# Last stage: the layer norm ahead of the feed-forward part with tokens on partitions, and call lists in another order

## The reference

```python
for i in range(DEPTH):
    x = attn_layer(shift_tokens(x), Wqkv[i], q_scale[i], k_scale[i], Wo[i]) + x
    x = ffn_layer(shift_tokens(x), ln_g[i], ln_b[i], W1[i], b1[i], W2[i], b2[i]) + x

def attn_layer(x, Wqkv, qs, ksc, Wo):      # 16 heads of 64
    q, k, v = split_heads(x @ Wqkv)
    q, k = l2norm(q) * qs, l2norm(k) * ksc
    q, k = rotary(q), rotary(k)            # with position scales
    out = local_attention(q, k, v)         # windows of 32, each sees itself and the one before
    return out @ Wo

def ffn_layer(x, g, bln, W1, b1, W2, b2):
    mu = x.mean(-1, keepdims=True)
    var = ((x - mu) ** 2).mean(-1, keepdims=True)
    xn = (x - mu) / jnp.sqrt(var + 1e-05) * g + bln
    a, gate = jnp.split(xn @ W1 + b1, 2, -1)
    return a * jax.nn.gelu(gate, approximate=False) @ W2 + b2
```

## Time and profile before

| | us |
|---|---|
| median of 3 runs | 4661.67 |
| lowest and highest | 4660.33 and 4680.19 |
| span of the profiled execution, first to last instruction | 4655.4 |

### The profile page before, as it was taken

The page is one execution under the profiler, slowest core; times in us unless marked ns, Lnnn a source line. Parts: engine busy times, 40 slices in busy tenths (PEclk is TensorE's granted clock), DMA queues, the critical chain, the costliest instruction groups (busy, mean ns, idle before and its releaser), DMA issues.

```text
span 4655.4 us, 137933 instructions
## 1 busy us (share of the span) xinstructions
PE 4360.4 (94%) x56640; PEld 2936.9 (63%) x56640; DVE 3703.2 (80%) x5128; ACT 3238.4 (70%) x6002; POOL 3648.6 (78%) x1951
## 2 busy tenths in 40 slices
PE   7889899978887999999999999999999999999998
PEld 4556688854443666666666666666666666666665
DVE  6874476759997888888888788888888788878885
ACT  4666655657774777777777777777777777777775
POOL 2223344469997999988999899989999898989993
PEclk9999999989998999999999999999999999999999
DMA  2000000023331222322233322323223222322222
GB/s 81 2 2 2 2 1 1 1 110 146 146 146 57 67 63 61 80 65 66 58 70 74 71 63 61 79 66 69 58 67 76 69 64 60 78 68 66 59 68 53
DMA packets 164376, 290.47 MB, mean 62 GB/s; under 512 B 44063, under 2 KB 61350, under 8 KB 159654
## 3 DMA queue, kind: packets, MB, share of 16 engines
q1 hardware_dynamic: 162310, 281.40, 23.2%
q10 hardware_dynamic: 1440, 0.24, 0.0%
HBM read 90.16 MB, written 2.62 MB: 20 GB/s over the span
## 4 chain that ended last, share of the span: by engine, by line
PE 57%; issue 4%; DVE 4%; DMA 2%; ACT 1%; SPq 1%; POOL 0%; DVEq 0%; ACTq 0%
PE ps L2626 19%; PE ps L2682 7%; PE ps L2639 7%; PE ps L2694 7%; PE ps L2655 5%; PE ps L2668 3%; PE ps L2720 3%; PE ps L2736 3%; PE ps L2727 3%; DMA L3f_vw<-L3f_v 2%; DVE L3f_ss L3019 1%; PE ps L2701 1%; PE ps L2707 1%; DVE L3f_raw L3036 1%; SPq L2472 1%
## 5 line engine op out<-in xcount | busy, mean ns | idle before, releaser
L3219 POOL TENSOR_TENSOR L3f_t<-L3f_raw,L3f_rot 128x1024 f32<-128x1024 f32 x384 | 1085.3, 2826 | 246.4 <-DVE L3f_raw L3036 242.8
L2626 PE MATMUL ps<-L3f_wqkv,all_z 128*128 128x512 f32 x2304 | 1154.1, 607 | 11.2 <-DVE L3f_raw L3036 8.8
L3236 POOL TENSOR_TENSOR L3f_raw<-L3f_raw,L3f_t 128x1024 f32<-128x1024 f32 x384 | 911.9, 2375 | 7.5
L3228 POOL TENSOR_TENSOR L3f_raw<-L3f_raw,L3f_rot 128x1024 f32<-128x1024 f32 x384 | 909.0, 2367 | 7.5
L2835 ACT ACTIVATE L3f_sqr<-ps 128x512 f32<-128x512 f32 x768 | 453.1, 595 | 295.8 <-PE ps L2626 292.4
L3036 DVE TENSOR_TENSOR L3f_raw<-ps,L3f_ri 128x512 f32<-128x512 f32 x768 | 498.7, 686 | 163.5 <-ACT L3f_ri L2845 154.4
L3019 DVE TENSOR_REDUCE L3f_ss<-L3f_sqr 128x8 f32<-128x512 f32 x768 | 515.6, 679 | 115.6 <-ACT L3f_sqr L2835 112.3
L2639 PEld LDWEIGHTS ps<-all_ident,L3f_raw 128*128 128x128 f32 x3072 | 363.3, 141 | 307.8 <-issue 270.3
L2626 PEld LDWEIGHTS ps<-L3f_wqkv,all_z 128*128 128x128 f32 x2304 | 395.8, 192 | 234.8 <-issue 180.2
L2639 PE MATMUL ps<-all_ident,L3f_raw 128*128 128x128 f32 x3072 | 474.5, 277 | 9.4 <-POOL L3f_raw L3236 3.7
L2682 PEld LDWEIGHTS ps<-L3f_pT,L3f_vw 128*64 128x64 f32 x12288 | 375.3, 138 | 97.0 <-issue 78.6
(11 more groups left out here) (332 smaller groups left out, 8632.4 us busy)
## 6 DMA issues: line engine op xcount, KB each, us to landing
L3f_vw<-L3f_v SPq DMA_DIRECT2D x1344, 128.0 KB, 2.4
L3a_Bs<-L3a_rows SPq DMA_DIRECT2D x16, 2048.0 KB, 7.1
L3a_Cs<-L3a_rows SPq DMA_DIRECT2D x16, 2048.0 KB, 11.7
L3f_vw<-L3f_v SPq DMA_DIRECT2D x192, 64.0 KB
L3f_wqkv<-in_L_ffn_Wqkv SPq DMA_DIRECT2D x24, 256.0 KB, 4.3
L3f_wqkv<-in_L_ffn_Wqkv SPq DMA_DIRECT2D x6, 512.0 KB, 4.2
L3f_wo<-in_L_ffn_Wo SPq DMA_DIRECT2D x48, 64.0 KB, 2.4
out<-all_x SPq DMA_DIRECT2D x8, 256.0 KB, 3.2
```

The source lines that it names most:

```text
L2626: p.matmul(PS[:, j % 3, :], Z[:, u % NSEQ, t * P:t * P + P], w, start=True, stop=True).then_inc(proj.sem)
L3219: g.tensor_tensor(t.rearrange("p h (b e) -> p h b e", b=2), r.rearrange("p h (b e) -> p h b e", b=2)[:, :, ::-1, :], w[:, 1, :].rearrange( ...
L3228: g.tensor_tensor(r, r, w[:, 0, :].unsqueeze(1).broadcast_to((P, H, HD)), ALU.mult).then_inc(cosined.sem)
L3236: g.tensor_tensor(r, r, t, ALU.add).then_inc(rotated.sem)
```

## The change

The norm ahead of the feed-forward part is computed with tokens on partitions. `turn_z` transposes the unit's two tiles of Z into the second half of bank 4; VectorE takes statistics (`stats`, `bn_stats` on each tile) and aggregates them into mean and variance per token (`moments`, `bn_aggr`); ScalarE takes logarithm and exponential of two values per partition (`root`); VectorE subtracts the mean and scales, both as values per partition (`normal`, two instructions, from PSUM into `zn`); `turn_n` transposes back into the same half bank; `affine` reads it from there. The constants `cmat` and `mean`, the products `centre` and `variance` and the square `centred` go. `turn_p` of the next unit now waits for `affine`. All call lists are in another order; the pairs of `pe` and `dve` are cut at another place of the period (`pe` now starts at `project_out(2i)`, `dve` at `residual(2i)`), and `pool` is written one pair ahead, with `add` of the odd unit's "q1" behind `sine` of its "k1". The diff, cut to its core:

```diff
-            def centre(u):
-                p.wait_ge(*z_attn.at(u))
-                p.matmul(PS[:, 4, SEQ:2 * SEQ], cmat[:, :], Z[:, u % NSEQ, 0:SEQ], start=True, stop=True).then_inc(c_mm.sem)
-            def variance(u):
-                p.wait_ge(*c_sq.at(u))
-                p.matmul(PS[:, 5, 0:SEQ], mean[:, :], xq[:, :], start=True, stop=True).then_inc(v_mm.sem)
+            def turn_z(u):
+                p.wait_ge(*z_attn.at(u))
+                for t in range(TILES):
+                    mm = p.transpose(PS[:, 4, SEQ + t * P:SEQ + (t + 1) * P], Z[:, u % NSEQ, t * P:(t + 1) * P], ident[:, :])
+                mm.then_inc(y_turned.sem)
+            def turn_n(u):
+                p.wait_ge(*y_n.all(u))
+                for t in range(TILES):
+                    mm = p.transpose(PS[:, 4, SEQ + t * P:SEQ + (t + 1) * P], zn[:, t, :], ident[:, :])
+                mm.then_inc(n_turned.sem)
...
-                    p.wait_ge(*fn_n.at(u - 1))
+                    p.wait_ge(*fn_in.at(u - 1))
...
             def root(u):
+                a.wait_ge(*y_mv.all(u))
+                a.activation(zls[:, :], zmv[:, :, 1], ACT.Ln, bias=self.eps[:, :]).then_inc(y_ln.sem)
+                a.wait_ge(*y_ln.at(u))
+                a.activation(zrs[:, :], zls[:, :], ACT.Exp, scale=-0.5).then_inc(y_rs.sem)
             def affine(u):
-                a.wait_ge(*fn_n.at(u))
+                a.wait_ge(*n_turned.at(u))
-                a.activation(fn[:, (u % 2) * SEQ:(u % 2 + 1) * SEQ], rs[:, :], ACT.Identity, bias=gb[:, y, 1:2], scale=gb[:, y, 0:1]).then_inc(fn_in.sem)
+                a.activation(fn[:, (u % 2) * SEQ:(u % 2 + 1) * SEQ], PS[:, 4, SEQ:2 * SEQ], ACT.Identity, bias=gb[:, y, 1:2], scale=gb[:, y, 0:1]).then_inc(fn_in.sem)
...
+            def stats(u):
+                    v.bn_stats(zst[:, t, :], PS[:, 4, SEQ + t * P:SEQ + (t + 1) * P]).then_inc(y_st.sem)
+            def moments(u):
+                    v.bn_aggr(zmv[:, t, :], zst[:, t, :]).then_inc(y_mv.sem)
             def normal(u):
-                v.tensor_tensor(rs[:, :], PS[:, 4, SEQ:2 * SEQ], rs[:, :], ALU.mult).then_inc(fn_n.sem)
+                    v.tensor_scalar(zn[:, t, :], PS[:, 4, SEQ + t * P:SEQ + (t + 1) * P], zmv[:, t, 0:1], zrs[:, t:t + 1], ALU.subtract, ALU.mult).then_inc(y_n.sem)
```

More of the change, by code:

```diff
@@ L2753, in turn_back @@
                     mm.then_inc(z_turned.sem)
+            project_out(2 * i)
+            ffn_gate(2 * i - 1, 1)
+            ffn_up(2 * i - 1, 0)
+            ffn_gate(2 * i - 1, 2)
+            project(2 * i + 2, "v1b")
+            turn_z(2 * i)
+            project(2 * i + 3, "q0a")
+            ffn_up(2 * i - 1, 1)
+            ffn_up(2 * i - 1, 2)
+            project(2 * i + 3, "q0b")
+            project(2 * i + 3, "k0a")
+            turn_qk(2 * i + 2, 0, 0)
+            turn_back(2 * i - 1, range(FINAL - 1))
+            ffn_out(2 * i - 1)
+            turn_back(2 * i - 1, range(FINAL - 1, FINAL))
+            turn_qk(2 * i + 2, 0, 1)
+            project(2 * i + 3, "k0b")
+            turn_n(2 * i)
+            turn_qk(2 * i + 2, 0, 2)
+            project(2 * i + 3, "v0a")
+            turn_qk(2 * i + 2, 0, 3)
+            turn_p(2 * i + 1, 0)
             turn_qk(2 * i + 2, 1, 0)
-            scores(2 * i + 2, 0)
             project(2 * i + 3, "v0b")
@@ L2778, in pe @@
             project(2 * i + 4, "k0a")
-            centre(2 * i + 1)
+            turn_z(2 * i + 1)
+            project(2 * i + 4, "k0b")
+            project(2 * i + 4, "v0a")
             turn_qk(2 * i + 3, 1, 0)
-            project(2 * i + 4, "k0b")
-            variance(2 * i + 1)
-            project(2 * i + 4, "v0a")
+            turn_n(2 * i + 1)
             scores(2 * i + 3, 0)
@@ L3160, in dve @@
             scale(2 * i + 1, 0)
-            total(2 * i + 1, 1)
-            residual(2 * i)
+            share(2 * i + 1, 1)
+            stats(2 * i)
             gated(2 * i - 1, 0)
+            moments(2 * i)
             gated(2 * i - 1, 1)
```

281 lines of the change are left out of this document (133 added, 148 removed).

## The result

The changed kernel takes 4687.75 us (median of 7 runs, 4677.23 to 4696.77), the kernel before beside it 4661.67 (7 runs, 4647.66 to 4680.19): ratio 1.0061, 95% interval 1.0041 to 1.0080. It is 0.6% slower. The prediction was 4634.5, 0.6% faster; the range, up to 4688.0, just holds the median, and that is luck: its upper end was set for short stalls of TensorE, which hardly came. The profiled execution has a span of 4691.6 us against 4655.4, 36.2 us apart where the medians are 26.1 apart.

What follows compares the result with a forecast made beforehand. TensorE's instruction stream was taken as the bound (63.79 us busy of a 63.98 us pair). Terms: -41.7 saving, +12 stalls, +10.5 layer boundaries, -8 rotation tables, sum -27: 4661.7 to 4634.5 us, range 4604 to 4688.

Steps and rivals of the forecast that it cites:

- The bound and the saving: TensorE's instruction stream bounds the last stage; products removed less transposes added save 0.87 us per pair, 41.7 us in all.
- New stalls: Short new TensorE waits in the new order, taken as 0.25 us per pair, 12 us in all; bounds -14 to +67.
- (a): VectorE's work after project_out(2i), up to the norm freeing the PSUM bank for "v0a": some 0.4 us in hand.
- (b): Between turn_z(2i+1) and turn_n(2i+1): statistics, root and scalings must fit into 2.15 us; stall 0 to 0.4 us.
- (c): turn_p(2i+1, 0) now waits for affine instead of normal, whose bank it overwrites; stall 0 to 0.3 us.
- second rival: TensorE's gain is given back in short waits at (a), (b) and (c): 43 us of stalls, 4665 us; chance 0.29.
- Rotation tables: Table preparation on VectorE, five times, now right before residual(2i): costs 1.5 instead of 3.1 us each, -8 us in all.
- Layer boundaries: At 5 boundaries project_out waits for output weights, 2.1 us longer each: +10.5 us; bounds 0 and +20.
- The failed step: Each of four softmax scalings per pair waits on VectorE for the rest of one GpSimd instruction, 0 to 2.2 us.
- third rival: Softmax scalings' waits for GpSimd decide: two of 2.2 us per pair, mean scaling up 0.3 us, 4733 us; chance 0.12.
- None of this has a price by itself: Changed loads of VectorE, ScalarE and GpSimd cost nothing, as none passes 63.1 us per pair; only order can cost.
- fourth rival: Longer transpose runs bring one slow clock stretch per pair on TensorE, 1.9 us each, 91 us: 4725 us; chance 0.03.

Runs made afterwards that it cites:

- new_norm_old_order: Kernel before with only the new norm (transposes, VectorE statistics); old call lists, only the new steps have new places: 4867.34 us, ratio 1.0438.
- a_pool_behind: Changed kernel with one more GpSimd wait: ahead of sine(2i+3, "k1") it waits until scale(2i+2, 0) is done: 4652.75 us, ratio 0.9982.
- the pads: Tiny transposes ahead of the stage: 32 or 64 on the changed kernel with scale(2i+1, 1) later, 4739.57 and 4727.70 us; 64 on the kernel before, 4658.84.
- a_behind_apart: a_pool_behind with scores(2i+2, 0) put back ahead of the products v0b, q1a, q1b on TensorE: 4798.37 us, ratio 1.0289.
- b_close: Kernel before with scores(2i+2, 0) moved behind the products v0b, q1a, q1b on TensorE: 4736.62 us, ratio 1.0165.
- n_tuned: new_norm_old_order with scale(2i, 0) three places ahead of residual(2i-1), root and normal earlier, turn_p(2i+3, 0) one turn later: 4704.45 us, ratio 1.0089.
- n_tuned_behind: n_tuned with GpSimd waiting for scale(2i, 0) ahead of sine(2i+2, "q0"): 4699.40 us, ratio 1.0085.

## Why the prediction was wrong, step by step

- **The bound and the saving** were right. An undisturbed pair took 63.8 us and takes 62.4 to 62.9 now. The steps cost what their rows said. Statistics took 0.284 us and aggregates 0.171; the two new scalings took 0.404 each where I had 0.281, and that did no harm. Most undisturbed pairs lie under 62.7, which by my own sign makes the prediction wrong: I had not seen that the wait of `turn_p` for `normal`, 10.6 us in all, would go.
- **New stalls at (a), (b), (c), +12 us**: over-sized. Between 1500 and 4550 us `turn_n` waits 0.8 us in all, `turn_z` about 2, and the projections 3.7 us in 4 places for a norm. So the second rival did not come, in these lists; new_norm_old_order shows how real it is where the list gives a chain no room.
- **Rotation tables, -8**: from W to W the five such pairs took 66.72 to 71.34 us before. They take 62.95, 67.29, 63.52, 65.57 and 63.75 now, the second and fourth with 2.6 and 2.4 us of fetch waits in them. Each had a wait at the residual, 0.9 to 2.5 us; one of 0.4 us is left. An estimate from these rows, fetch waits and the shorter ordinary pair taken off, is -10: right.
- **Layer boundaries, +10.5**: +7.0 in waiting. W behind the wait takes 5.2 to 6.4 us in four boundaries and 3.7 in one, where before it took 5.2 to 5.4 in each.
- **The failed step** is the sentence that each scaling waits "for the rest of a GpSimd instruction, 0 to 2.2 us". The earlier trace rows show one such case, and I made it the upper end. In the changed lists GpSimd often runs eight and more instructions without a break (each starts before the one ahead of it has ended) when `scale(2i+2, 0)` asks. Of some 42 scalings that met such a run, 8 lost the path to two to four further instructions; of some 230 in the two kernels that met a run of up to six, none did. This one mis-sized term cost 35 us (a_pool_behind), and it is the third rival's mechanism: the two engines' lock decides; but not by its price, two scalings of 2.2 us in every pair, and not by its sign that the mean would rise by 0.3 us (it rose by 0.17). With 0.12 its chance was too low, because I judged it by means and not by what a rare long one does. "None of this has a price by itself", said of GpSimd's unchanged work too, is where I stopped asking.
- **The missing term** is fetch. The waits view of before shows 32.8 us of TensorE waiting for issue at `scores` alone, nearly twice the 17.6 us at the layer boundaries, which I priced. I took the 80 us of idle in the stage for 0.19 us per pair, from one undisturbed window. Fetch grew by 20 us, and with the lower clock behind each wait it ate most of what was left of the gain: without the scalings the kernels are equal.
- **The clock**: "fourth rival, 0.03" was right for undisturbed pairs, at 1.00 with 24 groups of transposes and four more pairs of them. The price came another way: each wait is followed by products at a lower granted clock (0.95 over the pair of 69.90 us), and 41 us of removed work became 16.7 of busy time. I had counted waits at their own length only. The Trainium skill, "TensorE: Matmul & The Clock Gate", section "Part 4: PE-mode transpose", has transposes not count as busy for the clock; no undisturbed pair of this kernel shows that (clock 1.00 over 62.60 us), with more of them than before.

The Trainium skill, "SBUF — State Buffer", section "SBUF: two separate sides", has it that the shared pair of ports is locked for one whole instruction of whichever engine starts first, while the other blocks. The 3.33 us of the earlier trace rows agree. The 7.81 us don't: a waiting VectorE instruction was passed over twice by GpSimd instructions that started after it asked, at 2239.95 and 2242.27 (three times in three other pairs, four times at 1507.08). The measurement decides here; the section's price of one instruction is no upper bound.

**What stays open.** Why the blocks of instructions are asked for later in the changed kernel. Shown not to be it: the number of instructions (the same), where blocks begin (the pads), the softmax scalings (fetch is 56.8 us without them). Closeness of the score groups is made unlikely (a_behind_apart, b_close). n_tuned and n_tuned_behind, with one TensorE list and 51.3 and 41.6 us, point to how far ahead TensorE's sequencer can run between waits, but no run isolates that. Nor is shown why a GpSimd run of eight lets VectorE in at once in most cases and passes it over in others; where it does, the wait ends as a rule at the next step at which GpSimd needs its own last result.

## What to carry to other kernels

A lock between two engines is priced by its longest wait, not by the length of one instruction: where an engine runs many instructions back to back, a small wait that lets the other one in can be worth nearly as much as the arithmetic saved (35 us for one line here, beside 41 us of products). Before reordering a list that is 97% full, add up all idle time of its bound engine over the whole stage, waits for issue too, and not in one good window. And look for a softmax or other shared-port instruction inside each short chain: one of 2.9 us in the norm's chain is the likely cause of most of 163 us.
